# A two-layer transformer kernel: third normalisation, denominators and values reordered by halves on ScalarE and TensorE

## The chip, the cores and the metric

The kernel runs on one core of one Trainium2 chip. Time is device microseconds (us) of one launch; the time before is the median of three runs. A core has TensorE (PE, matrix products and transposes; PEld are its weight loads), VectorE (DVE), ScalarE (ACT), GpSimd (POOL) and SyncE (SP, which only issues DMAs here). The engines run their own instruction queues in order and wait for each other on semaphores.

## The reference, cut to what matters

32 independent items x[b] of 128 x 1024 pass through four residual stages, each behind a layer norm:

```python
x = x + _L0_xattn_ref(_layernorm(x), ctx_4096, ...)  # attention over 1024 positions
x = x + _L0_ffn_ref(_layernorm(x), ...)              # routed feed-forward, sign weights
x = x + _L1_xattn_ref(_layernorm(x), ctx_4096, ...)  # attention, 128 keys
x = x + _L1_ffn_ref(_layernorm(x), ...)              # routed low-rank feed-forward

# L0_xattn: q, k of 64 rows from ctx; attention = softmax(q k) over 1024 x 1024
v = jnp.einsum('oc,bct->bto', Wv, x) + bv
out = jnp.einsum('bts,bsc->bct', attention, v)
# L1_ffn
router_logits = jnp.einsum('bsd,hd->bsh', x, Wr) + br
scores = H * jax.nn.softmax(router_logits, axis=-1)
low = jnp.einsum('bsd,hrd->bshr', x, A)
out = SCALING * jnp.einsum('bshr,hor,bsh->bso', low, B, scores)
```

All is computed in float32, or in pairs of float32r parts (hi and lo) that together carry it.

## The kernel before, in words

After a setup of constants (transposed, split and multiplied weights) the kernel works on three items at a time, in a software pipeline. The body of iteration k does three kinds of work: **prepare** item b = k (load it, transpose its context, queries and keys, values), **attend** to item a = k-1 (the 1024 x 1024 attention of the first stage, in eight steps s), and **chain** for item c = k-2 (the second to fourth stages). `iterations` runs k = 0, 1, 2 written out, k = 3 to 31 in a loop, and k = 32 (attend and chain) and k = 33 (chain alone) written out. So thirty bodies, k = 2 to 31, hold all three kinds.

The order on each engine is the order in which its `body` is written; there is no scheduler. PSUM is full: `scores[0]`, `scores[1]`, `acc` (two banks each) and `shared[0]`, `shared[1]` (one bank each) pass from one use to the next, and the semaphores guard these passes.

The stretch that matters is the end of a body, after the last of the eight attention steps (line numbers are those of the kernel before):

- TensorE: transposes of `den_inv`, the reciprocal denominators, into `scores[1]` (L1192); transposes of the context `c_in` into `shared` (L1004), four per half; transposes of `xn_3`, the input of the fourth stage, into `shared` (L1004 again; `xn_3` is the buffer `p_sum`); `values(0)` and `values(1)` (L1010), eight small products of `xn` and `wvT` into `scores[1]`, four per half; the low-rank product with the router (L1213, `low_done`); first products of the next item's `kw` (L1037 to L1039); the transpose of `low` (L1219); the output products (L1224 to L1230). In this list a float32 matmul shows as two instructions.
- ScalarE: `den_rows` (the buffer `prob[0]`) from `scores[1]`, both halves (L729); `cT_hi` (L733); the third normalisation into `xn_3`, 1024 wide (`normalize(3, ...)`, L643); `cT_whole` (L740); the first half of `xnT` (L649); `v_hi` by halves (L748, L750); the router's exponential (L753).
- VectorE: statistics for the third normalisation (L774 to L779); `den_inv` (L935); `cT_lo` (L944); `x1_half(a, 0)` (L801, L802); the second half of `xnT` (L790); `x1_half(a, 1)`; statistics for the first normalisation of the attended item (L774 on); the router's softmax (L962 to L966) and `low` (L968).
- GpSimd turns the statistics into `rstd` and `shift` (`norm_scale`, L617, L618).

`half(h)` is the h-th 512 columns. `nth(per, b, n)` is the semaphore value after n of item b's `per` increments.

Of the kernel before, what the change touches and what calls it, by code (L numbers as in the profile page):

```python
# [21 lines left out]
ACT = mybir.ActivationFunctionType  # L22
# [26 lines left out]
def build(nc, x, ctx_, wq0, bq0, wk0, bk0, wv0, bv0, w_ffn, b_ffn, gate, ics, ocs,  # L49
# [13 lines left out]
    with top:  # L63
        def sb(name, shape, dt=F32, stack=top):
            return stack.enter_context(nc.sbuf_tensor(name, shape, dt))

        def sem(name, stack=top):
            return stack.enter_context(nc.semaphore(name))
# [36 lines left out]
        with ExitStack() as tmp:  # L105
# [62 lines left out]
            with nc.Block() as block:  # L168
                @block.sync
                def _(sp):  # L170
                    for i in range(4):
                        sp.dma_start(wq_nat[:, 2 * i:2 * i + 2, :],
                                     wq1[2 * i * P:(2 * i + 2) * P, :].rearrange("(t p) x -> p t x", p=P)).then_inc(wq_in[i], 16)
                    for i in range(2):
                        sp.dma_start((wf_first, wf_last)[i][:, :, :],
                                     w_ffn[4 * i * P:(4 * i + 4) * P, :].rearrange("(t p) h -> p t h", p=P)).then_inc(wf_in[i], 16)
                    for n, ft in enumerate(f_order):
                        sp.dma_start(of_tile(ft, wk_nat_split, wk_nat_whole),
                                     wk1[:, ft * P:(ft + 1) * P].rearrange("(t p) f -> p t f", p=P)).then_inc(wk_in[n], 16)
# [238 lines left out]
        den_rows = prob[0]  # L418
        unread = prob[1]

        res = sb("res", [P, D])
# [9 lines left out]
        rstd = [sb(f"rstd{i}", [P, 1]) for i in range(4)]  # L431
        shift = [sb(f"shift{i}", [P, 1]) for i in range(4)]
# [22 lines left out]
        def psum(name, shape):  # L455
            return top.enter_context(nc.psum_tensor(name, shape, F32))

        scores = [psum(f"scores{i}", [P, D]) for i in range(2)]
# [13 lines left out]
        shift_ready = [sem(f"shift_ready{i}") for i in range(4)]  # L472
        normed = [sem(f"normed{i}") for i in range(4)]
# [10 lines left out]
        den_done = sem("den_done")  # L484
        den_turned = sem("den_turned")
# [33 lines left out]
        den_rows_ready = sem("den_rows_ready")  # L519
        x1_ready = sem("x1_ready")  # L520
# [33 lines left out]
        def half(h):  # L554
            return slice(h * HALF, (h + 1) * HALF)
# [5 lines left out]
        def nth(per, b, n):  # L561

            if isinstance(b, int):
                return max(0, per * min(b, NB - 1) + n)
            return b * per + n


        def iterations(engine, body):  # L570
            for k in range(3):
                body(k, True, k >= 1, k >= 2)
            with engine.Fori(3, NB) as k:
                body(k, True, True, True)
            body(NB, False, True, True)
            body(NB + 1, False, False, True)

        with nc.Block() as block:
# [31 lines left out]
            @block.gpsimd  # L610
            def _(pool):
                def norm_scale(i, b):

                    pool.wait_ge(var_ready[i], nth(1, b, 1))
                    pool.wait_ge(normed[i], nth(1, b - 1, 1))
                    pool_norm[i].begin(b)
                    pool_norm[i].chain(pool, nc.gpsimd.tensor_tensor(rstd[i][:, :], var_eps[i][:, :], minus_half[:, :], ALU.pow))  # L617
                    nc.gpsimd.tensor_tensor(shift[i][:, :], neg_mean[i][:, :], rstd[i][:, :], ALU.mult).then_inc(shift_ready[i], 1)  # L618
                    pool_norm[i].end()

                def body(k, prepare, attend, chain):
                    b, a, c = k, k - 1, k - 2
                    if chain:
                        pool.wait_ge(x1_ready, nth(2, c, 2))
                        pool.wait_ge(out_ready, nth(2, c - 1, 2))
                        nc.gpsimd.tensor_tensor(res[:, :], x1[:, :], bias_rows[:, :], ALU.add).then_inc(biased, 1)
                    if chain:
                        norm_scale(2, c)
                    if prepare:
                        norm_scale(0, b)  # L630
                    if chain:
                        norm_scale(3, c)
                    if attend:
                        norm_scale(1, a)

                iterations(pool, body)
# [3 lines left out]
            def _(act):  # L640
                def normalize(i, b, to, src):
                    act.wait_ge(shift_ready[i], nth(1, b, 1))
                    nc.scalar.activation(to[:, :], src[:, :], ACT.Identity, bias=shift[i][:, :],  # L643
                                         scale=rstd[i][:, :]).then_inc(normed[i], 1)

                def transposed_half(i, c):

                    act.wait_ge(xnT_done[i], nth(2, c, 1))
                    nc.scalar.activation(tile4(xnT, 0), shared[0][:, :], ACT.Identity).then_inc(xnT_a_ready[i], 1)  # L649

                def body(k, prepare, attend, chain):
                    b, a, c = k, k - 1, k - 2
# [32 lines left out]
                    for s in range(T):  # L685
# [14 lines left out]
                        if chain and s == 3:  # L700
                            act.wait_ge(x2_ready, nth(2, c, 2))
                            normalize(2, c, xn_2, res)
# [15 lines left out]
                    if prepare:  # L718
                        for h in range(2):
                            act.wait_ge(qk_done, nth(2, b, h + 1))  # L720
                            nc.scalar.activation(q_hl[0:DQK, half(h)], scores[0][0:DQK, half(h)], ACT.Identity,
                                                 bias=bqk_col[0:DQK, :]).then_inc(q_hi_ready, 1)
                            nc.scalar.activation(k_hh[DQK:P, half(h)], scores[0][DQK:P, half(h)], ACT.Identity,
                                                 bias=bqk_col[DQK:P, :]).then_inc(k_hi_ready, 1)
                    if attend:
                        for h in range(2):
                            act.wait_ge(den_turned, nth(2, a, h + 1))
                            act.wait_ge(x1_ready, nth(2, a - 1, 2))
                            nc.scalar.activation(den_rows[:, half(h)], scores[1][:, half(h)], ACT.Identity).then_inc(den_rows_ready, 1)  # L729
                    if prepare:  # L730
                        act.wait_ge(cT_done, nth(2, b, 1))
                        act.wait_ge(kw_done, nth(2, b - 1, 2))
                        nc.scalar.activation(cT_hi[:, :, :].rearrange("p t c -> p (t c)"), shared[0][:, :],  # L733
                                             ACT.Identity).then_inc(cT_hi_ready, 1)
                    if chain:
                        act.wait_ge(den_done, nth(1, a, 1))
                        normalize(3, c, xn_3, res)
                    if prepare:
                        act.wait_ge(cT_done, nth(2, b, 2))
                        nc.scalar.activation(cT_whole[:, :, :].rearrange("p t c -> p (t c)"), shared[1][:, :],  # L740
                                             ACT.Identity).then_inc(cT_whole_ready, 1)
                    if chain:
                        act.wait_ge(sc1_done, nth(1, c, 1))
                        transposed_half(3, c)
# [251 lines left out]
            def _(pe):  # L996
# [3 lines left out]
                def transposes(h, src, semaphore):  # L1000

                    for j in range(4):
                        t = 4 * h + j
                        last = nc.tensor.transpose(shared[h][:, j * P:(j + 1) * P], src[:, t * P:(t + 1) * P], ident[:, :])  # L1004
                    last.then_inc(semaphore, 1)

                def values(h):

                    for t in range(4 * h, 4 * h + 4):
                        last = mm(scores[1][:, t * P:(t + 1) * P], xn[:, t * P:(t + 1) * P], wvT[:, :], start=True, stop=True)  # L1010
                    last.then_inc(v_done, 1)
# [71 lines left out]
                def body(k, prepare, attend, chain):  # L1083
                    b, a, c = k, k - 1, k - 2
# [110 lines left out]
                    if prepare:  # L1195
                        for h in range(2):
                            pe.wait_ge(x3_ready, nth(2, c, h + 1))
                            transposes(h, c_in, cT_done)
                    if chain:
                        pe.wait_ge(normed[3], nth(1, c, 1))  # L1200
                        for h in range(2):
                            pe.wait_ge((cT_lo_ready, cT_whole_ready)[h], nth(1, b, 1))
                            transposes(h, xn_3, xnT_done[3])
                    if prepare:
                        pe.wait_ge(normed[0], nth(1, b, 1))
                        pe.wait_ge(den_rows_ready, nth(2, a, 2))
                        values(0)
                        values(1)
                    if chain:
                        pe.wait_ge(xnT_a_ready[3], nth(1, c, 1))  # L1210
                        pe.wait_ge(xnT_b_ready[3], nth(1, c, 1))
# [44 lines left out]
```

## Time and profile before

| | us |
|---|---|
| median of three runs | 2334.17 (2333.06 to 2336.49) |
| profiled execution | 2332.57 |
| its span | 2330.8 |
| PE busy | 2175.6 (93%) |
| DVE busy | 1874.4 (80%) |
| ACT busy | 1113.5 (48%) |
| POOL busy | 260.2 (11%) |

The mean granted clock of TensorE over the span was 0.979 of full speed. Busy shares are means over the span. A wait shows in the trace as idle time ahead of an instruction, in square brackets with the instruction that released it. TensorE's matmuls are pipelined: the next one's start lies before the last one's end. The chain of waits is the sequence of work, one piece released by the other, that leads to the last instruction.

### The profile page before, as it was taken

The numbers are of one execution on the slowest core, as the hardware profiler recorded it, in microseconds if no ns is written. First come the engines' busy times: TensorE is split into PE (matmuls) and PEld (weight loads), VectorE is DVE, ScalarE is ACT, GpSimd is POOL, SyncE is SP. The second block draws the span as 40 slices with busy tenths as digits, with TensorE's granted clock in tenths as the row PEclk, the third lists the DMA queues.
The fourth block names the chain that finished last, engine by engine and source line by source line (L and its number), as shares of the span: only waits on it lengthen the run. The fifth ranks groups of instructions, "written<-read, shape, count | busy, mean of one in ns | idle before, by whom it ended". The sixth has DMA issues, their size and how long they took to land.

```text
span 2330.8 us, 34027 instructions
## 1 busy us (share of the span) xinstructions
PE 2175.6 (93%) x11166; PEld 1668.0 (72%) x11166; DVE 1874.4 (80%) x3130; ACT 1113.5 (48%) x1625; POOL 260.2 (11%) x302
## 2 busy tenths in 40 slices
PE   1997999999999999999999999999999999999996
PEld 0784777777777777777777777777777777777774
DVE  1436888988888888898888888898888888888873
ACT  1103545555555554555555544555555555455541
POOL 0000111111011111111011111111101111111100
PEclk7999999999999999999999999999999999999996
DMA  8001111111111111111111111111111111111100
GB/s 241 10 1 45 46 55 37 54 54 49 41 54 45 45 54 46 44 54 54 36 54 49 46 50 54 36 54 54 48 42 54 45 45 54 41 49 54 54 10 27
DMA packets 50217, 115.58 MB, mean 50 GB/s; under 512 B 14800, under 2 KB 23248, under 8 KB 50192
## 3 DMA queue, kind: packets, MB, share of 16 engines
q1 hardware_dynamic: 38624, 113.26, 14.8%
q10 hardware_dynamic: 11568, 1.98, 0.6%
q8 instruction: 16, 0.26, 0.0%
q14 instruction: 9, 0.07, 0.0%
HBM read 81.67 MB, written 16.78 MB: 42 GB/s over the span
## 4 chain that ended last, share of the span: by engine, by line
PE 85%; ACT 4%; issue 2%; DVE 2%; DMA 0%; POOL 0%; ACTq 0%; SPq 0%; POOLq 0%; DVEq 0%
PE acc L1080 15%; PE acc L1041 10%; PE scores L1024 5%; PE shared L1004 5%; PE shared L1054 5%; PE shared L1055 5%; PE scores L1069 5%; PE scores L1068 5%; PE shared L1213 3%; PE shared L1171 3%; PE acc L1037 3%; PE acc L1039 3%; PE acc L1038 3%; PE shared L1155 3%; PE scores L1182 2%; PE scores L1010 2%
## 5 line engine op out<-in xcount | busy, mean ns | idle before, releaser
L892 DVE TENSOR_TENSOR p_lo<-prob,p_hi 128x1024 fp32r<-128x1024 f32 x256 | 312.1, 1219 | 106.5 <-ACT p_hi L699 88.5
L692 ACT ACTIVATE prob<-scores 128x1024 f32<-128x1024 f32 x256 | 260.7, 1018 | 228.8 <-PE scores L1069 177.7
L785 DVE TENSOR_REDUCE neg_max<-scores 128x1 f32<-128x1024 f32 x256 | 312.0, 1219 | 38.1 <-PE scores L1024 32.7
L617 POOL TENSOR_TENSOR rstd<-var_eps,minus_half 128x1 f32<-128x1 f32 x128 | 127.0, 992 | 1883.7 <-DVE var_eps L779 1883.7
L699 ACT ACTIVATE p_hi<-prob 128x1024 fp32r<-128x1024 f32 x256 | 271.4, 1060 | 42.8 <-PE acc L1080 38.6
L1041 PE MATMUL acc<-m_whole,cT_whole 128*128 128x512 f32 x512 | 255.8, 601 | 0.0
L900 DVE TENSOR_TENSOR p_sum<-p_sum,prob 128x1024 f32<-128x1024 f32 x192 | 233.7, 1217 | 0.0
L1054 PE MATMUL shared<-signT,y_hi 128*128 128x512 f32 x512 | 206.6, 404 | 0.4 <-ACT oscale L681 0.4
L1068 PE MATMUL scores<-q_hl,k_hh 128*128 128x512 f32 x512 | 201.6, 394 | 1.8 <-DVE q_m L874 1.4
L1055 PE MATMUL shared<-signT,y_lo 128*128 128x512 f32 x512 | 202.5, 396 | 0.0
L1024 PE MATMUL scores<-k_hh,q_hl 128*128 128x512 f32 x512 | 202.3, 476 | 0.3 <-issue 0.3
L1069 PE MATMUL scores<-q_m,k_l 128*128 128x512 f32 x512 | 201.8, 394 | 0.0
L1080 PE MATMUL acc<-p_hi,v_hi 128*128 128x512 f32 x512 | 170.8, 415 | 4.1 <-DVE p_lo L892 3.9
L1080 PE MATMUL acc<-p_lo,v_hi 128*128 128x512 f32 x512 | 161.1, 395 | 0.0
L1080 PE MATMUL acc<-p_hi,v_lo 128*128 128x512 f32 x512 | 161.0, 395 | 0.0
L1024 PEld LDWEIGHTS scores<-k_hh,q_hl 128*128 128x128 f32 x512 | 94.2, 189 | 65.0 <-issue 46.6
L1004 PE MATMUL shared<-ident,p_sum 128*128 128x128 f32 x512 | 70.9, 283 | 57.5 <-ACT p_sum L643 57.5
L1041 PEld LDWEIGHTS acc<-m_whole,cT_whole 128*128 128x128 f32 x512 | 89.6, 189 | 44.3 <-issue 36.8
L1054 PEld LDWEIGHTS shared<-signT,y_hi 128*128 128x128 f32 x512 | 97.2, 190 | 26.8 <-DVE y_lo L808 0.9
L1068 PEld LDWEIGHTS scores<-q_hl,k_hh 128*128 128x128 f32 x512 | 96.1, 188 | 25.8 <-DVE q_m L874 1.8
L1037 PE MATMUL acc<-m_hi,cT_hi 128*128 128x512 f32 x256 | 109.5, 428 | 4.1 <-DVE cT_lo L944 2.2
L1080 PEld LDWEIGHTS acc<-p_lo,v_hi 128*128 128x128 f32 x512 | 96.0, 188 | 23.5
(221 smaller groups left out, 4301.4 us busy)
## 6 DMA issues: line engine op xcount, KB each, us to landing
c_in<-in_ctx SPq DMA_DIRECT2D x32, 512.0 KB, 3.3
xn<-in_x SPq DMA_DIRECT2D x32, 512.0 KB, 4.1
x<-in_x SPq DMA_DIRECT2D x32, 512.0 KB, 3.3
c_val<-in_ctx SPq DMA_DIRECT2D x32, 512.0 KB, 3.5
out_x<-oscale SPq DMA_DIRECT2D x32, 512.0 KB, 2.9
q_m<-q_hl SPq DMA_DIRECT2D x32, 256.0 KB, 3.1
k_hh<-k_hh SPq DMA_DIRECT2D x32, 256.0 KB, 3.4
wq_nat<-in_L_xattn_Wq SPq DMA_DIRECT2D x4, 1024.0 KB, 10.0
```

The source lines that it names most:

```text
L692: nc.scalar.activation(prob[s % 2][:, :], scores[s % 2][:, :], ACT.Exp).then_inc(exp_ready, 1)
L699: nc.scalar.activation(p_hi[s % 2][:, :], prob[s % 2][:, :], ACT.Identity).then_inc(p_hi_ready, 1)
L785: nc.vector.tensor_reduce(neg_max[:, t:t + 1], scores[t % 2][:, :], AX_X, ALU.max, negate=True).then_inc(row_max, 1)
L892: nc.vector.tensor_tensor(p_lo[s % 2][:, :], prob[s % 2][:, :], p_hi[s % 2][:, :].bitcast(F32), ALU.subtract).then_inc(p_lo_ready, 1)
L900: nc.vector.tensor_tensor(p_sum[:, :], p_sum[:, :], prob[s % 2][:, :], ALU.add).then_inc(p_summed, 1)
L1024: last = mm(scores[t % 2][:, half(h)], q_hl[:, t * P:(t + 1) * P], k_hh[:, half(h)], start=True, stop=True)
L1041: last = mm(acc[:, half(h)], cT_whole[:, f - TS, :], m_whole[:, f - TS, half(h)], start=f == 0, stop=f == T - 1)
L1054: mm(shared[h][:, :], y_hi[:, f, :], signT[:, f, half(h)], start=f == 0, stop=False)
L1055: last = mm(shared[h][:, :], y_lo[:, f, :], signT[:, f, half(h)], start=False, stop=f == T - 1)
L1068: mm(scores[s % 2][:, half(h)], k_hh[:, s * P:(s + 1) * P], q_hl[:, half(h)], start=True, stop=False)
L1069: last = mm(scores[s % 2][:, half(h)], k_l1[:, s * P:(s + 1) * P], q_m[:, half(h)], start=False, stop=True)
L1080: last = mm(acc[:, half(h)], v[:, s, :], p[s % 2][:, half(h)], start=first, stop=end)
```

## The change

ScalarE normalises `xn_3` in two halves of 512 columns. The first half comes ahead of the first half of the denominators' eviction, the second between `cT_hi` and `cT_whole`; the second half of the denominators comes behind `cT_whole`. TensorE computes `values(0)` ahead of the transposes of `xn_3` and `values(1)` behind them, each waiting for its own half of `den_rows`, and each half of the transposes waits for its own half of `xn_3`. The semaphore `normed[3]` now counts two per item, and GpSimd's wait on it follows.

```diff
@@ norm_scale, GpSimd
-                    pool.wait_ge(normed[i], nth(1, b - 1, 1))
+                    pool.wait_ge(normed[i], nth(2, b - 1, 2) if i == 3 else nth(1, b - 1, 1))
@@ helpers, ScalarE
+                def normalize_half(i, b, h, to, src):
+                    act.wait_ge(shift_ready[i], nth(1, b, 1))
+                    nc.scalar.activation(to[:, half(h)], src[:, half(h)], ACT.Identity, bias=shift[i][:, :],
+                                         scale=rstd[i][:, :]).then_inc(normed[i], 1)
+
+                def evict_den(a, h):
+                    act.wait_ge(den_turned, nth(2, a, h + 1))
+                    act.wait_ge(x1_ready, nth(2, a - 1, 2))
+                    nc.scalar.activation(den_rows[:, half(h)], scores[1][:, half(h)], ACT.Identity).then_inc(den_rows_ready, 1)
@@ body, ScalarE
-                    if attend:
-                        for h in range(2):
-                            act.wait_ge(den_turned, nth(2, a, h + 1))
-                            act.wait_ge(x1_ready, nth(2, a - 1, 2))
-                            nc.scalar.activation(den_rows[:, half(h)], scores[1][:, half(h)], ACT.Identity).then_inc(den_rows_ready, 1)
+                    if chain:
+                        act.wait_ge(den_done, nth(1, a, 1))
+                        normalize_half(3, c, 0, xn_3, res)
+                    if attend:
+                        evict_den(a, 0)
                     if prepare:
                         ...
                     if chain:
-                        act.wait_ge(den_done, nth(1, a, 1))
-                        normalize(3, c, xn_3, res)
+                        normalize_half(3, c, 1, xn_3, res)
                     if prepare:
                         ...
+                    if attend:
+                        evict_den(a, 1)
@@ values, TensorE
-                def values(h):
-
+                def values(h, a):
+                    pe.wait_ge(den_rows_ready, nth(2, a, h + 1))
@@ body, TensorE
-                    if chain:
-                        pe.wait_ge(normed[3], nth(1, c, 1))
+                    if prepare:
+                        pe.wait_ge(normed[0], nth(1, b, 1))
+                        values(0, a)
+                    if chain:
                         for h in range(2):
+                            pe.wait_ge(normed[3], nth(2, c, h + 1))
                             pe.wait_ge((cT_lo_ready, cT_whole_ready)[h], nth(1, b, 1))
                             transposes(h, xn_3, xnT_done[3])
                     if prepare:
-                        pe.wait_ge(normed[0], nth(1, b, 1))
-                        pe.wait_ge(den_rows_ready, nth(2, a, 2))
-                        values(0)
-                        values(1)
+                        values(1, a)
```

ScalarE's order in the loop's body before, from the last eviction of the keys on (`prob` is `den_rows`, `p_sum` is `xn_3`):

```order
L723 ACTIVATE k_hh<-scores,bqk_col 64x512
L729 ACTIVATE prob<-scores 128x512 [waits x1_ready,den_turned] x2
L733 ACTIVATE cT_hi<-shared 128x512 [waits kw_done,cT_done]
L643 ACTIVATE p_sum<-res,shift,rstd 128x1024 [waits shift_ready3,den_done]
L740 ACTIVATE cT_whole<-shared 128x512 [waits cT_done]
L649 ACTIVATE xnT<-shared 128x512 [waits xnT_done3,sc1_done]
```

And after the change:

```order
L733 ACTIVATE k_hh<-scores,bqk_col 64x512
L648 ACTIVATE p_sum<-res,shift,rstd 128x512 [waits shift_ready3,den_done]
L654 ACTIVATE prob<-scores 128x512 [waits x1_ready,den_turned]
L743 ACTIVATE cT_hi<-shared 128x512 [waits kw_done,cT_done]
L648 ACTIVATE p_sum<-res,shift,rstd 128x512 [waits shift_ready3]
L749 ACTIVATE cT_whole<-shared 128x512 [waits cT_done]
L654 ACTIVATE prob<-scores 128x512 [waits x1_ready,den_turned]
L659 ACTIVATE xnT<-shared 128x512 [waits xnT_done3,sc1_done]
```

One instruction of 1024 columns became two of 512, and the two denominators' evictions moved apart.

TensorE's order at the same place before, from the transposes of the context to the low-rank product:

```order
L1004 MATMUL shared<-ident,c_in 128x128 [waits x3_ready]
L1004 MATMUL shared<-ident,c_in 128x128 x3
L1004 MATMUL shared<-ident,p_sum 128x128 [waits cT_lo_ready,normed3]
L1004 MATMUL shared<-ident,p_sum 128x128 x3
L1004 MATMUL shared<-ident,p_sum 128x128 [waits cT_whole_ready]
L1004 MATMUL shared<-ident,p_sum 128x128 x3
L1010 MATMUL scores<-wvT,xn 128x128 [waits den_rows_ready,normed0]
L1010 MATMUL scores<-wvT,xn 128x128 x7
L1213 MATMUL shared<-lowT,xnT 128x136 [waits xnT_b_ready3,xnT_a_ready3]
```

And after:

```order
L1015 MATMUL shared<-ident,c_in 128x128 [waits x3_ready]
L1015 MATMUL shared<-ident,c_in 128x128 x3
L1021 MATMUL scores<-wvT,xn 128x128 [waits den_rows_ready,normed0]
L1021 MATMUL scores<-wvT,xn 128x128 x3
L1015 MATMUL shared<-ident,p_sum 128x128 [waits cT_lo_ready,normed3]
L1015 MATMUL shared<-ident,p_sum 128x128 x3
L1015 MATMUL shared<-ident,p_sum 128x128 [waits cT_whole_ready,normed3]
L1015 MATMUL shared<-ident,p_sum 128x128 x3
L1021 MATMUL scores<-wvT,xn 128x128 [waits den_rows_ready]
L1021 MATMUL scores<-wvT,xn 128x128 x3
L1224 MATMUL shared<-lowT,xnT 128x136 [waits xnT_b_ready3,xnT_a_ready3]
```

Half of the values moved ahead of the eight transposes, and one more wait stands in the row. VectorE's and SyncE's orders are as before.

## Rows read from the trace of the kernel before

**Rows 1.** The page, busy us, share of the span and instructions of each engine
```profile
PE 2175.6 (93%) x11166; PEld 1668.0 (72%) x11166; DVE 1874.4 (80%) x3130; ACT 1113.5 (48%) x1625; POOL 260.2 (11%) x302
```

**Rows 2.** The chain of waits, 1017 to 1036 us: start, us, what
```profile
1025.61 1.79 PE scores L1010 x16
1027.40 1.86 PE shared L1213 x16
1029.25 0.23 PE acc L1037
...
1031.35 0.11 PE shared L1219
```

**Rows 3.** Waits of the whole run: total us, times, longest
```profile
PE shared L1004 <- ACT p_sum L643: 57.5, 32, 4.9
```

**Rows 4.** Instructions in order of time, TensorE, 1009 to 1035 us
```profile
1021.79 1.04 PE L1004 MATMUL shared<-ident,c_in 128*128 128x128 f32 x8
1024.52 1.09 PE L1004 MATMUL shared<-ident,p_sum 128*128 128x128 f32 x8 [1.70 <-ACT p_sum L643]
```

**Rows 5.** The same, ScalarE
```profile
1021.55 1.09 ACT L729 ACTIVATE prob<-scores 128x512 f32<-128x512 f32 x2 [1.67 <-PE scores L1192]
1022.52 0.60 ACT L733 ACTIVATE cT_hi<-shared 128x512 fp32r<-128x512 f32 x1
1023.15 1.24 ACT L643 ACTIVATE p_sum<-res,shift,rstd 128x1024 f32<-128x1024 f32 x1
1024.30 0.58 ACT L740 ACTIVATE cT_whole<-shared 128x512 f32<-128x512 f32 x1
1025.27 0.60 ACT L649 ACTIVATE xnT<-shared 128x512 f32<-128x512 f32 x1 [0.40 <-PE shared L1004]
```

**Rows 6.** The same, VectorE
```profile
1023.16 0.69 DVE L944 TENSOR_TENSOR cT_lo<-shared,cT_hi 128x512 fp32r<-128x512 f32 x1 [1.48 <-ACT cT_hi L733]
...
1024.48 0.75 DVE L802 SCALAR_TENSOR_TENSOR x<-prob,bv_col,x 128x512 f32<-128x512 f32 x1
1025.65 0.69 DVE L790 COPY xnT<-shared 128x512 f32<-128x512 f32 x1 [0.42 <-PE shared L1004]
...
1029.47 0.16 DVE L962 TENSOR_TENSOR logit<-shared,br_rows 128x8 f32<-128x8 f32 x1
...
1030.76 0.29 DVE L968 TENSOR_TENSOR low<-shared,route 128x128 f32<-128x128 f32 x1
```

**Rows 7.** The same, GpSimd
```profile
1020.84 0.19 POOL L618 TENSOR_TENSOR shift<-neg_mean,rstd 128x1 f32<-128x1 f32 x1
```

**Rows 8.** Groups by line and shape, ScalarE: busy us, mean ns, idle before
```profile
L699 ACT ACTIVATE p_hi<-prob 128x1024 fp32r<-128x1024 f32 x256 | 271.4, 1060 | 42.8 <-PE acc L1080 38.6
...
L643 ACT ACTIVATE p_sum<-res,shift,rstd 128x1024 f32<-128x1024 f32 x32 | 39.7, 1240 | 6.4 <-POOL shift L618 5.6
...
L676 ACT ACTIVATE y_hi<-xnT 128x512 fp32r<-128x512 f32 x64 | 39.3, 631 | 72.2 <-DVE xnT L861 72.2
```

**Rows 9.** Instructions in order of time, last body (k = 33), GpSimd and ScalarE
```profile
2313.16 0.19 POOL L618 TENSOR_TENSOR shift<-neg_mean,rstd 128x1 f32<-128x1 f32 x1
2313.44 1.24 ACT L643 ACTIVATE p_sum<-res,shift,rstd 128x1024 f32<-128x1024 f32 x1 [5.63 <-POOL shift L618]
```

**Rows 10.** The same, body k = 32, TensorE
```profile
2258.05 1.91 PE L1192 MATMUL scores<-ident,den_inv 128*128 128x128 f32 x8
2261.77 1.97 PE L1004 MATMUL shared<-ident,p_sum 128*128 128x128 f32 x8 [1.81 <-ACT p_sum L643]
2264.61 3.83 PE L1213 MATMUL shared<-lowT,xnT 128*128 128x136 f32 x16 [0.87 <-DVE xnT L790]
```

**Rows 11.** The same, VectorE
```profile
2263.78 0.69 DVE L790 COPY xnT<-shared 128x512 f32<-128x512 f32 x1 [2.43 <-PE shared L1004]
```

**Rows 12.** Stretches: us, busy (instructions) of PE, PEld, DVE, ACT, POOL, PEclk, DMA
```profile
1021.00:1025.00 4.00, 2.30 (x21) 2.07 (x20) 2.49 (x5) 3.30 (x5) 0.02 (x1) 1.00 0.31 87
2260.00:2265.00 5.00, 2.35 (x10) 1.99 (x11) 2.53 (x4) 2.32 (x3) 0.00 (x0) 0.50 0.00 0
```

## The prediction

> **What bounds the kernel now.** I read the page first. TensorE is busy for 93% of the span and VectorE for 80% [rows 1]. A change that takes no work away can gain only where TensorE stands idle, or where VectorE hands it something late. The waits of the whole run say where: the transposes of `xn_3` wait for ScalarE's normalisation in all 32 bodies, 57.5 us together [rows 3]. In a body of the loop that is one gap of 1.70 us, from the end of the context's transposes at 1022.83 to 1024.52 [rows 4]. It is the only long gap of a body, and the change is aimed at it. Thirty bodies (k = 2 to 31) have all three kinds of work and show this stretch alike; the two after them differ and are priced apart.
>
> Then the order of time on each engine, to see who is late. ScalarE evicts the denominators from 1021.55 (it had idled 1.67 us), `cT_hi` from 1022.52, normalises from 1023.15 to 1024.39, and `cT_whole` follows at 1024.30 [rows 5]. TensorE starts 0.13 us after the normalisation's end; that is the hand-over I use. The shift that the normalisation needs was ready at 1021.03 [rows 7], two microseconds earlier: it waits only for its turn on ScalarE.
>
> The chain of waits then stays on TensorE: transposes, values (1.79 us), low-rank product (1.86), first products for the next item from 1029.25, the transpose of `low` from 1031.35 [rows 2]. But VectorE is close beside it. From `cT_lo` on, its only idle time up to the router is 0.42 us ahead of its copy of the second half of `xnT` at 1025.65 [rows 6]. After that come `x1_half`, the statistics and the router without a gap until `logit` at 1029.47, and `low` ends at 31.05 (1030.76 + 0.29), just 0.3 us before its transpose [rows 2, 6]. So whatever TensorE wins in front of `low`, it loses again waiting for `low`, unless VectorE becomes earlier too. That decides the size of the gain.
>
> **The change part by part**, at the body around 1023; all times from here are us behind 1000.
>
> *First half on ScalarE.* In the last body the shift ends at 2313.35 and the normalisation starts at 2313.44 [rows 9], so the first half starts at 21.03 + 0.09 = 21.12. The trace has no normalisation of 512 columns. A plain copy from SBUF takes 1060 ns for 1024 columns and 631 for 512; the normalisation takes 1240 for 1024, 180 more than the plain copy [rows 8]. I take 631 + 180 = 0.81 us. Bounds: 0.62 (half of 1.24, no fixed part) and 1.24 (no gain from the halving). Neighbours on ScalarE overlap by 0.09 (24.30 against 24.39) [rows 5]. So the denominators' first half starts at 21.12 + 0.81 - 0.09 = 21.84 instead of 21.55; two of them started 0.97 apart from `cT_hi` [rows 5], so one takes 0.49, and `cT_hi` could start at 22.33. It needs the first four transposes of `c_in`, which start at 21.79 [rows 4]; four transposes reach ScalarE after 0.75 us (24.52 to 25.27) [rows 4, 5], that is at 22.54. So `cT_hi` keeps its start, 22.52, with 0.2 us of cover, and costs nothing. Without that cover (a half over 1.0 us) everything behind moves by the excess.
>
> *VectorE ahead of the transposes.* `cT_lo` waits for `cT_hi` and stays at 23.16. `x1_half(a, 0)` follows it and ends at 25.23 as before [rows 6]; its half of the denominators is ready at about 22.4, its cover is `cT_lo`.
>
> *`values(0)` on TensorE.* Half of 1.79, 0.90 us, starts at once at 22.83 (denominators' half 0 evicted by then) and ends at 23.73. The transposes' first half waits for `cT_lo` as before, 23.85 + 0.13 = 23.98. So `values(0)` lies wholly in the old gap and delays nothing.
>
> *Second half on ScalarE and second transposes.* The normalisation's second half starts at 23.15 and ends at 23.96, `cT_whole` runs from 23.87 to 24.45, and the second transposes, which wait for it, start at 24.58, against about 25.15 before. If they start on an idle engine, VectorE sees them 0.75 later, at 25.33; if they follow the first four without a break (these end at about 24.60), VectorE sees them 1.13 after 23.98, as before (24.52 to 25.65), at 25.11 [rows 4, 6]. VectorE is free at 25.23. So its copy starts at 25.23 to 25.33 instead of 25.65: 0.32 to 0.42 earlier, and I take 0.37.
>
> The Trainium skill speaks against halving: "Advanced Engine Details and Errata", section "The Read-Write Bubble", says that on ScalarE and VectorE the memory latency is exposed between instructions, so that large tiles are cheaper. The two plain copies agree: 2 x 631 - 1060 = 202 ns are paid per instruction [rows 8]. With that fixed part the half is 0.81 and the end is 25.33; without it the half is 0.62 and VectorE's own 25.23 binds. It costs at most 0.1 us a body, since only one half lies on the path.
>
> *Behind the transposes.* The denominators' second half runs on ScalarE from 24.36 to 24.96, `values(1)` from about 25.09 to 26.0, and `xnT` is whole on VectorE at 25.28 + 0.69 = 25.97. The low-rank product starts at about 26.1 and not 27.40: TensorE is here 1.3 us early. `x1_half(a, 1)` needs the denominators' second half at 25.9, which is covered. TensorE's first products (2.1 us, 29.25 to 31.35) then end at 26.1 + 1.86 + 2.1 = 30.06. But VectorE's row is only 0.37 earlier: `low` ends at 30.68, its transpose starts at about 30.8. TensorE idles some 0.7 us there. So of 1.3 us it keeps about 0.4: the gap of 1.70 is split, not filled, and what is late next is `low`. After that both engines run as before, 0.37 earlier, into the next body, where every wait is for TensorE or VectorE themselves. The semaphore's new count on GpSimd is met long before it is asked for.
>
> *Body k = 32.* There is no `cT_hi` or `values`. The transposes started at 2261.77 behind ScalarE's row; the denominators' transposes ended at 2259.96. The first half of the normalisation is done by then, the second by about 2260.5. TensorE can go on at about 2260.0, and the copy of `xnT` that started at 2263.78 comes at about 2262.1: 1.7 us [rows 10, 11]. Bounds: 0 and 1.81, the gap. *Body k = 33:* the transposes start after 0.81 instead of 1.24 [rows 8, 9]: 0.4 us.
>
> *Sum.* 30 x 0.37 + 1.7 + 0.4 = 13.2 us. The profiled execution took 2332.57, so it would take 2319.4. The median of the runs shown is 1.6 above it, 2334.17, so I predict 2321.0. The two ends of the forecast's own term are 0.25 (a hand-over or a restart of TensorE more than counted) and 0.50 (VectorE's 0.42, and the transpose of `low` no longer queued behind a matmul): 9.6 and 17.1 us, so 2325 and 2317.
>
> **The rivals.**
>
> *The second transposes are not earlier (no change).* They wait for `cT_whole`, which still stands behind a normalisation half. For 0.32 us of gain the half must take 0.81; at 1.0 us VectorE is at 25.52 and the gain is 0.13 a body, 30 x 0.13 + 1.5 = 5 us: 2329. For it speaks that the half was never measured; against it, 631 ns for the plain copy. 2329 to 2334.
>
> *TensorE keeps all of its lead.* If `low` didn't bind, a body would gain 1.3 us: 30 x 1.3 + 2 = 41, 2293. Against it stands VectorE's gapless row from 25.65 to `logit` [rows 6].
>
> *Slower: halves that cost as much as the whole.* At 1.24 us each, the denominators start at 22.27, `cT_hi` at 22.76 (0.24 late), `cT_lo` follows, the second half of the normalisation runs 23.39 to 24.63, `cT_whole` to 25.12, the second transposes start at 25.25, and VectorE copies at 26.00 instead of 25.65. That is 30 x 0.35 = 10.5 us, less about 1 in the last bodies: 2344. It turns into a loss from a half of about 1.07 us on. Only the 1024-wide row supports it; the 631 ns speak against it [rows 8].
>
> *Slower: TensorE's clock.* The gap becomes several short ones. In the present body the clock stays at 1.00 (2.4 GHz) through a gap of 1.70 us [rows 12]. In k = 32 it is 0.50 (1.2 GHz) [rows 12], and it had fallen before that body's gap of 1.81: the eight transposes ahead of it took 1.91 us, eight of the same shape in the loop 1.04 [rows 4, 10]. At the lower level transposes take 1.97 against 1.09 and the low-rank product 3.83 against 1.86 [rows 2, 4, 10]; with values at twice 1.79 that is 9.4 us from 22.83, 32.2 instead of 29.25, 3.0 us a body: 2334 + 89 = 2423. Idle time in the stretch gets less, not more, so I give it little. The Trainium skill has such a case in "TensorE: Matmul & The Clock Gate", section "A second HAM failure mode: psum-queue depth-cycling": short idles between groups of matmuls made the clock go up and down.
>
> **How the numbers follow.** Forecast 75%, the second transposes not earlier 13%, TensorE keeps all 3%, costly halves 5%, clock 4%. The 0.2% that a measurement of this kernel can tell from no change is 4.7 us. Of the 13% about 6 still gain more than that. So faster is 75 + 3 + 6 = 84%, within 0.2% 8%, slower 8% (the last two rivals, less a mild form of either). Range: the forecast's own 2317 to 2325, widened below to 2314 for a stretch that gains 0.6 a body, above to 2329 for a half of 1.0 us.
>
> **What would show it.** In the profile after: the normalisation in halves of about 810 ns; `cT_hi` and `cT_lo` at the same distance as now; the idle time ahead of VectorE's copy of `xnT` down from 0.42 to about 0.1; the low-rank product about 1.3 us earlier against `cT_hi`, the transpose of `low` only about 0.4; a new wait of TensorE for `low`, 0.6 to 0.7 us in thirty bodies, some 20 us in all; and TensorE's wait for `xn_3` near nothing in the loop. I am wrong in size if `logit` no longer follows the statistics without a gap, or if the second transposes come later than 25.2; wrong in sign if a half takes over 1.07 us or the clock in the loop falls below 1.00.

## The result and the profile after

The changed kernel takes 2312.55 us (median of four runs, 2311.51 to 2312.75) against 2335.16 us for the kernel before in the same session (2333.06 to 2336.49). The ratio is 0.9907, 95% interval 0.9894 to 0.9919: 21.7 us less, where 13.2 were forecast. The sign was right; the time lies 1.5 us below the range.

The profiled execution has a span of 2310.7 us, 20.1 less than before. Here is where they are, taken at the start of `cT_hi` on ScalarE, which every body with prepare has once:

| us | before | after |
|---|---|---|
| start to `cT_hi` of k = 2 | 305.98 | 309.54 |
| from there to k = 31 (29 bodies) | 1889.36 | 1871.62 |
| one of these bodies | 65.15 | 64.54 |
| from there to the end | 135.43 | 129.54 |

The bodies with all three kinds of work are 0.61 us shorter each, not 0.37; in either kernel the 29 intervals lie within 0.1 us of each other. The first and last bodies move by several us in opposite directions; more on them below.

TensorE in the body around 1020, in order of time (start us, us, engine, line, operation, shapes, count, idle before and its releaser); it answers to [rows 4] and [rows 2]:

```profile
1017.91 1.04 PE L1203 MATMUL scores<-ident,den_inv 128*128 128x128 f32 x8
1018.78 1.04 PE L1015 MATMUL shared<-ident,c_in 128*128 128x128 f32 x8
1019.70 1.13 PE L1021 MATMUL scores<-wvT,xn 128*128 128x128 f32 x8
1020.91 1.09 PE L1015 MATMUL shared<-ident,p_sum 128*128 128x128 f32 x8
1021.84 1.09 PE L1021 MATMUL scores<-wvT,xn 128*128 128x128 f32 x8
1022.90 2.09 PE L1224 MATMUL shared<-lowT,xnT 128*128 128x136 f32 x16
...
1027.50 0.33 PE L1230 MATMUL shared<-ident,low 128*128 128x128 f32 x1 [0.41 <-DVE low L979]
```

The low-rank product and `low`'s transpose in the kernel before, whose denominators' transposes start at 1020.92:

```profile
1027.23 2.02 PE L1213 MATMUL shared<-lowT,xnT 128*128 128x136 f32 x16
...
1031.19 0.27 PE L1219 MATMUL shared<-ident,low 128*128 128x128 f32 x1
```

The gap of 1.70 us is gone. From the start of the denominators' transposes to that of the low-rank product it is now 4.99 us and was 6.31, but a new wait of 0.41 us stands ahead of `low`'s transpose. ([rows 2], and with them the prediction, have 1027.40 and 1031.35. Those are starts of pieces of the chain, which begin where the matmul ahead ends; the instructions themselves start 0.17 and 0.16 earlier.) The transposes of `xn_3` run as one group of eight: the second four did not start anew.

ScalarE, for [rows 5]:

```profile
1018.12 0.81 ACT L648 ACTIVATE p_sum<-res,shift,rstd 128x512 f32<-128x512 f32 x1 [1.24 <-POOL shift L618]
1018.96 0.60 ACT L654 ACTIVATE prob<-scores 128x512 f32<-128x512 f32 x1
1019.45 0.59 ACT L743 ACTIVATE cT_hi<-shared 128x512 fp32r<-128x512 f32 x1
1019.93 0.81 ACT L648 ACTIVATE p_sum<-res,shift,rstd 128x512 f32<-128x512 f32 x1
1020.63 0.60 ACT L749 ACTIVATE cT_whole<-shared 128x512 f32<-128x512 f32 x1
1021.11 0.61 ACT L654 ACTIVATE prob<-scores 128x512 f32<-128x512 f32 x1
```

A half takes 0.81 us, as worked out. But `cT_hi` comes 1.54 us behind the denominators' transposes and not 1.60, and the second half overlaps `cT_hi`'s end by 0.11, where the whole normalisation had started 0.03 behind it [rows 5].

VectorE, for [rows 6]:

```profile
1020.07 0.69 DVE L955 TENSOR_TENSOR cT_lo<-shared,cT_hi 128x512 fp32r<-128x512 f32 x1 [1.39 <-ACT cT_hi L743]
...
1021.40 0.75 DVE L813 SCALAR_TENSOR_TENSOR x<-prob,bv_col,x 128x512 f32<-128x512 f32 x1
1022.07 0.68 DVE L801 COPY xnT<-shared 128x512 f32<-128x512 f32 x1
...
1025.87 0.16 DVE L973 TENSOR_TENSOR logit<-shared,br_rows 128x8 f32<-128x8 f32 x1
...
1026.69 0.16 DVE L976 RECIPROCAL r_inv<-r_sum 128x1 f32<-128x1 f32 x1 [0.46 <-ACT r_exp L764]
...
1027.15 0.29 DVE L979 TENSOR_TENSOR low<-shared,route 128x128 f32<-128x128 f32 x1
```

There is no bracket left ahead of the copy of `xnT`: VectorE's row is without a gap from `cT_lo` to `logit`. The copy starts 0.08 before its neighbour ends (1022.15). In the chain of waits of this stretch (start us, us, what), TensorE has handed over to VectorE:

```profile
1019.55 0.50 ACT cT_hi L743
...
1020.68 0.69 DVE prob L812
...
1021.40 0.69 DVE x L813
1022.09 0.66 DVE xnT L801
...
1027.15 0.30 DVE low L979
...
1027.50 0.33 PE shared L1230
```

Before, ScalarE's normalisation and then TensorE alone stood there, up to `low`'s transpose:

```profile
1023.15 1.25 ACT p_sum L643
...
1024.52 1.09 PE shared L1004 x8
```

In the whole run VectorE has 9% of the chain now and had 2%.

How VectorE's row reaches the next body is seen at its end. The values' remainders (`v_lo`) are read out of `scores[1]`, and TensorE's next product into `scores[1]`, which belongs to the next body, waits for them. VectorE, TensorE's weight load, and that wait in the whole run:

```profile
1029.37 1.29 DVE L994 TENSOR_TENSOR v_lo<-scores,v_hi 128x512 fp32r<-128x512 f32 x2
1030.72 0.19 PEld L1035 LDWEIGHTS scores<-k_hh,q_hl 128*128 128x128 f32 x1 [0.30 <-DVE v_lo L994]
PEld scores L1035 <- DVE v_lo L994: 9.3, 31, 0.5
```

### The profile page after: what moved, and what is told of

It is laid out like the page before. It is cut to its first block, busy times and chain, and to the rows that moved or that the text cites. A ratio compares the mean times of both kernels' runs of the same rounds, so it can differ in the third digit from the quotient of the medians.

```text
span 2310.7 us, 34120 instructions
## 1 busy us (share of the span) xinstructions
PE 2193.5 (95%) x11166; PEld 1672.1 (72%) x11166; DVE 1872.3 (81%) x3130; ACT 1116.4 (48%) x1657; POOL 259.9 (11%) x302
## 4 chain that ended last, share of the span: by engine, by line
PE 77%; DVE 9%; issue 3%; ACT 2%; POOL 0%; DMA 0%; DVEq 0%; SPq 0%; POOLq 0%; ACTq 0%
PE acc L1091 15%; PE acc L1052 10%; PE scores L1035 5%; PE shared L1065 5%; PE shared L1066 5%; PE scores L1080 5%; PE scores L1079 5%; PE shared L1015 4%; PE shared L1182 3%; PE shared L1166 3%; PE scores L1193 2%; PE scores L1187 2%; DVE x L813 2%; DVE prob L812 2%; PE acc L1048 2%
## 5 line engine op out<-in xcount | busy, mean ns | idle before, releaser
L1080 PEld LDWEIGHTS scores<-q_m,k_l 128*128 128x128 f32 x512 | 96.1, 188 | 23.0
```

Source lines behind the costliest of these rows:

```text
L1080: last = mm(scores[s % 2][:, half(h)], k_l1[:, s * P:(s + 1) * P], q_m[:, half(h)], start=False, stop=True)
```

## The experiments

All are compared with the kernel before, run beside them: it took 2333.20 us beside e1 to e4, 2334.07 beside e5 to e8, and 2334.84 beside e9 and e10. "A body" is the mean over the 29 intervals from k = 2 to 31 in the profile. The last two columns are distances from the start of the denominators' transposes in the body around 1020.

| | median us | ratio (95%) | a body | copy of `xnT` | `low` |
|---|---|---|---|---|---|
| before | 2335.16 | | 65.15 | 4.73 | 9.84 |
| after | 2312.55 | 0.9907 (0.9894 to 0.9919) | 64.54 | 4.16 | 9.24 |
| e1_act_only | 2313.43 | 0.9918 (0.9905 to 0.9932) | 64.54 | 4.15 | 9.24 |
| e2_pe_only | 2332.43 | 0.9997 (0.9988 to 1.0006) | 65.10 | 4.71 | 9.80 |
| e3_pad_after | 2323.59 | 0.9958 (0.9944 to 0.9971) | 64.86 | 4.48 | 9.57 |
| e4_pad_before | 2333.81 | 1.0004 (0.9995 to 1.0013) | 65.14 | 4.74 | 9.83 |
| e7_whole_ahead | 2327.03 | 0.9972 (0.9961 to 0.9983) | 64.97 | 4.58 | 9.67 |
| e8_halves_behind | 2336.97 | 1.0014 (1.0005 to 1.0023) | 65.34 | 4.95 | 10.05 |
| e5_router | 2301.67 | 0.9859 (0.9843 to 0.9875) | 64.23 | 4.14 | 8.56 |
| e6_router_before | 2345.36 | 1.0052 (1.0038 to 1.0065) | 65.50 | 4.74 | 9.84 |
| e9_router_values_late | 2323.29 | 0.9955 (0.9941 to 0.9968) | 64.90 | 4.15 | 9.23 |
| e10_stats_later | 2303.86 | 0.9867 (0.9852 to 0.9883) | 64.25 | 4.15 | 8.58 |

**Which part does it: e1_act_only and e2_pe_only.** Each half of the change alone.

```diff
@@ e1, from after, TensorE: values back behind the transposes
-                        values(0, a)
                     if chain: ... transposes(h, xn_3, xnT_done[3])
                     if prepare:
+                        values(0, a)
                         values(1, a)
@@ e2, from before, TensorE: values(0, a) ahead, values(1, a) behind, ScalarE untouched
```

> The kernel after, but with both halves of the values behind the transposes of xn_3 on TensorE, as before the change; ScalarE's new order and its halves stay. Theory: VectorE's gapless row sets the gain as long as TensorE stays in front of it. TensorE's part is then 0.90 us later at the low-rank product: in the profile after it would end its first products at 1027.75 instead of waiting until 1027.50 for low, so 0.25 to 0.35 us a body are lost: 2312.5 + 9 = 2321 (2318 to 2324). Rival 1, only ScalarE's order counts: 2312 to 2314. Rival 2, the gain is the TensorE work that was put into the gap (0.9 us a body): the gain is gone, 2334 to 2339.

> The kernel before, with TensorE's part of the change alone: the first half of the values ahead of the transposes of xn_3, each half waiting for its own half of the denominators. ScalarE as before. Theory: VectorE's copy of xnT still waits for the whole normalisation, low is as late as before, so at most 0.1 us a body: 2332 to 2336. Rival 1 (only ScalarE's order counts): the same, 2335. Rival 2, the filled gap is the gain: 0.9 us x 30 = 27 less, 2308.

The first expectation missed (2318 to 2324 us, measured 2313.43). The low-rank product is 0.72 us later than in the kernel after, as it had to be, and the body is the same to 0.01 us. Its profile, TensorE in order of time:

```profile
1017.00 1.03 PE L1203 MATMUL scores<-ident,den_inv 128*128 128x128 f32 x8
...
1022.71 2.02 PE L1223 MATMUL shared<-lowT,xnT 128*128 128x136 f32 x16
...
1026.66 0.28 PE L1229 MATMUL shared<-ident,low 128*128 128x128 f32 x1
```

`low`'s transpose comes 9.66 behind the start against 9.59: TensorE just arrives when `low` does. So TensorE's half of the change, which fills the gap one sees, is worth nothing by itself: in the loop 0.003 us a body on top of ScalarE's half, and 0.05 alone, which the timed runs cannot tell from nothing (0.9988 to 1.0006). In e2 the low-rank product is 0.77 us earlier than in the kernel before (5.54 against 6.31), and TensorE loses it in a wait for `low`:

```profile
1032.73 0.33 PE L1219 MATMUL shared<-ident,low 128*128 128x128 f32 x1 [0.41 <-DVE low L968]
```

Rival 2, that the work put into the gap is the gain, is refuted in both directions. Rival 1, that only ScalarE's order counts, holds in both kernels.

**Is VectorE's row the bound: e3_pad_after and e4_pad_before.** The same addition in both kernels, ahead of the copy of `xnT`:

```diff
+                    if prepare and chain:
+                        nc.vector.tensor_tensor(pad[:, :], bias_rows[:, 0:256], bias_rows[:, 0:256], ALU.add)
                     if chain:
                         transposed_half(3, c)
```

> The kernel after, with one more addition of 256 columns on VectorE (about 0.35 us) ahead of the copy of the second half of xnT, in the thirty bodies of all three kinds. Theory: VectorE's row is the bound, so it costs its whole length, 30 x 0.3 to 0.4 = 9 to 12 us: 2322 to 2325. Rival, TensorE or ScalarE is the bound in this stretch: 0 to 2 us, 2312 to 2315.

> The kernel before, with the same added addition of 256 columns on VectorE. Theory: VectorE waits 0.42 us there for TensorE's transposes, and a released instruction misses another 0.08 of overlap with its neighbour, so an addition of 0.35 us is hidden: 0 to 2 us, 2335 to 2337. Rival, VectorE was the bound already before the change: 9 to 12 us, 2344 to 2347.

In the profile of e3 the addition, in order of time on VectorE, takes its slot:

```profile
1024.10 0.75 DVE L814 SCALAR_TENSOR_TENSOR x<-prob,bv_col,x 128x512 f32<-128x512 f32 x1
1024.77 0.42 DVE L964 TENSOR_TENSOR pad<-bias_rows 128x256 f32<-128x256 f32 x1
1025.10 0.68 DVE L802 COPY xnT<-shared 128x512 f32<-128x512 f32 x1
```

It moves the copy by 0.33 us and the body by 0.32 (64.54 to 64.86). Before the change it costs nothing measurable (65.15 to 65.14). Both costs are as expected; e4's time lies 1.2 us under the range given for it because the kernel before, beside it, took 2333.20 and not 2335; the difference is 0.6. The change put the part of VectorE's row ahead of the copy on the path, and the slack that it used up was at least 0.33 us.

**Which of ScalarE's moves: e7_whole_ahead and e8_halves_behind.** Early but whole; halved but not early.

```diff
@@ e7, from after, ScalarE (and the counts of normed[3] back to one)
-                        normalize_half(3, c, 0, xn_3, res)
+                        normalize(3, c, xn_3, res)
...
-                        normalize_half(3, c, 1, xn_3, res)
@@ e8, from after, ScalarE
-                        normalize_half(3, c, 0, xn_3, res)
                         evict_den(a, 0)
                         ... cT_hi ...
+                        normalize_half(3, c, 0, xn_3, res)
                         normalize_half(3, c, 1, xn_3, res)
```

> The kernel after, but the third normalisation is one instruction of 1024 columns again, where its first half stood (ahead of the denominators' first half); all the rest as after. Theory (what counts is when VectorE's row starts, by cT_hi, and that the second transposes are ready when it is free): the normalisation holds ScalarE from 18.12 to 19.36 in the profile after, cT_hi comes at about 19.88 instead of 19.45, so VectorE's row is 0.4 us later; a body takes 64.9 to 65.0 us instead of 64.54, the kernel 2322 to 2327. Rival, only the early start of the normalisation counts: 2312 to 2315.

> The kernel after, but both halves of the normalisation stand behind cT_hi and ahead of cT_whole; the denominators' first half is ahead of cT_hi again, their second half last. Theory: cT_hi is as early as after, but cT_whole and with it the second transposes wait for two halves, about 1.4 us behind cT_hi's end, and VectorE copies xnT at about the distance of before: a body of 65.0 to 65.2 us, 2330 to 2336. Rival, the halving itself or the late second half of the denominators is the gain: 2312 to 2320.

e7, ScalarE in order of time:

```profile
1019.92 1.24 ACT L643 ACTIVATE p_sum<-res,shift,rstd 128x1024 f32<-128x1024 f32 x1 [1.24 <-POOL shift L618]
1021.19 0.60 ACT L654 ACTIVATE prob<-scores 128x512 f32<-128x512 f32 x1
1021.68 0.59 ACT L743 ACTIVATE cT_hi<-shared 128x512 fp32r<-128x512 f32 x1
```

`cT_hi` starts 1.76 us behind the normalisation's start instead of 1.33: 0.43 later, and the body is 0.43 longer than after. It keeps 0.18 of the 0.61 us, as its expectation said (64.9 to 65.0 us a body). e8 has `cT_hi` early, but the copy of `xnT` waits again, on VectorE:

```profile
1026.61 0.69 DVE L800 COPY xnT<-shared 128x512 f32<-128x512 f32 x1 [0.73 <-PE shared L1014]
```

Its body is 0.19 longer than before. Body and time had been expected at 65.0 to 65.2 and 2330 to 2336 us, and lie 0.14 and 1 us above the upper ends. So neither an early normalisation nor a halved one is the gain by itself: the halves pay because one of them fits into ScalarE's idle time ahead of the denominators without delaying `cT_hi`.

In the eight kernels in which VectorE's row behind the copy is the same (before, after, e1 to e4, e7, e8), the body is the copy's distance plus 60.38 to 60.42 us. In all twelve it is the distance from the denominators' transposes to the end of the values' remainders (a mean over the bodies) plus 51.77 to 51.81 us, although that distance goes from 12.46 (e5) to 13.73 (e6), and TensorE's product into `scores[1]` starts 0.05 to 0.06 us behind that end. So the end of VectorE's row sets the body, before the change and after it.

**What binds behind the copy: e5_router and e6_router_before.** VectorE's order, from after and from before; nothing is left out:

```diff
                         dve.wait_ge(x1_ready, nth(2, a, 2))
-                        statistics(dve_attend, 1, a, x1)
+                        first half of bn_stats
                         logit, its maximum
+                        second half of bn_stats   (while ScalarE does the exponential)
                         reciprocal, route1, low
+                        bn_aggr, neg_mean, var_eps
```

> The kernel after, with VectorE's row behind x1_half(a, 1) reordered and nothing left out: first half of the statistics, then logit and its maximum, then the second half of the statistics while ScalarE does the exponential, then the rest of the router with low, then the end of the statistics. Theory: low, not TensorE, is what is late, so low is about 0.6 us earlier (27.15 to 26.5 in the profile after), and 0.46 us of VectorE's waiting for the exponential are filled: TensorE keeps 0.3 to 0.45 us a body, 2299 to 2304. Rival, the end of VectorE's row (the values' remainders) or TensorE is the bound and low was not: 2310 to 2314.

> The kernel before, with the same reordering of VectorE's row. Theory: before the change the low-rank product ends at 1029.25, later than logit would now be asked for (about 1028.5), so VectorE waits and low comes at most 0.1 us earlier; TensorE was no later than low there: at most 0.15 us a body, 2329 to 2334. Rival, VectorE's row is the bound with or without the change: 0.3 to 0.45 us a body, 2320 to 2325.

e5 is the fastest kernel of the study, 2301.67 us, some 11 us below the kernel after. On VectorE the wait for the exponential is filled and `logit` waits 0.16 for the low-rank product:

```profile
1022.35 0.69 DVE L795 BATCH_NORM_STATS2 stat<-x 128x6 f32<-128x512 f32 x1
1023.21 0.17 DVE L985 TENSOR_TENSOR logit<-shared,br_rows 128x8 f32<-128x8 f32 x1 [0.16 <-PE shared L1242]
1023.41 0.16 DVE L986 TENSOR_REDUCE r_max<-logit 128x1 f32<-128x8 f32 x1
1023.49 0.68 DVE L797 BATCH_NORM_STATS2 stat<-x 128x6 f32<-128x512 f32 x1
1024.21 0.16 DVE L991 RECIPROCAL r_inv<-r_sum 128x1 f32<-128x1 f32 x1
```

`low` is 0.68 us earlier, its transpose 0.59 (9.00 against 9.59), but the body only 0.31: the values' remainders at the end of VectorE's row, which TensorE waits for in the next body, start 0.30 earlier (11.16 against 11.46). So the end of the row counts and not `low`. The expectation met the time (2299 to 2304) and the 0.3 us a body, but not for the reason it gave, that `low` is what is late: the body follows the row's end. e6 shows it from the other side, and its expectation missed in sign. `logit` finds the low-rank product not done:

```profile
1036.40 0.17 DVE L974 TENSOR_TENSOR logit<-shared,br_rows 128x8 f32<-128x8 f32 x1 [0.84 <-PE shared L1231]
```

`low` is where it was (9.84), and yet the body is 0.35 longer: the waiting time in the row, 0.84 us, outweighs what is filled (0.46), and the start of the row's last two operations is 0.37 late (12.43 against 12.06). The kernel is 11 us slower than before, where up to 5 us less had been expected.

**When does the order of the values pay: e9_router_values_late; and the rest of the row: e10_stats_later.** e9 is e5 with both halves of the values behind the transposes (TensorE's part of the diff of e1). e10 is e5 with `bn_aggr, neg_mean, var_eps` behind the remainder of `lowT`.

> The kernel after with VectorE's reordered row (router between the halves of the statistics), and both halves of the values behind the transposes on TensorE, as before the change. Theory: in this row logit is asked for about 0.7 us earlier, so the 0.7 us by which the order of the values moves the low-rank product is no longer hidden: logit waits for it, VectorE's row and a body are 0.4 to 0.7 us longer than with the values split (64.23), 64.6 to 64.9, the kernel 2313 to 2322. Rival, the order of the values never matters (it moved the body by 0.003 us under the old row): 2300 to 2304.

> The kernel after with VectorE's reordered row, and the last three small operations of the statistics moved behind the remainder of lowT. Theory: VectorE's row has the same length, so its end (the values' remainders) stays and with it the body, 64.2; only TensorE's wait of about 0.12 us for lowT's remainder goes: 0 to 0.1 us a body, 2298 to 2303. Rival, low's transpose and the output products are the bound and not the row's end: 0.12 to 0.4 us a body, 2290 to 2298.

e9's body is 0.67 us longer than e5's (64.90 against 64.23), the upper end of the expectation, and its time, 2323.29 us, 1.3 us above it: `logit` waits again, on VectorE,

```profile
1028.88 0.17 DVE L985 TENSOR_TENSOR logit<-shared,br_rows 128x8 f32<-128x8 f32 x1 [0.81 <-PE shared L1241]
```

The same order of the values that was worth 0.003 us a body under the old row is worth 0.67 under the new one. e10 is no better than e5 (64.25 against 64.23 a body; its 2303.86 us are 0.9 above the range): TensorE's last short wait in front of the output products was not on the path.

## Why the prediction was right in sign and wrong in size

*The gap and what takes its place.* Right. The 1.70 us are gone, the low-rank product is early (4.99 against 6.31 us behind the denominators' transposes, 1.3 earlier, as forecast), and half of it is lost again: `low`'s transpose is only 0.69 earlier. The wait for `low` is 0.41 us in the trace's bracket, 0.6 to 0.7 forecast, since `low` itself came 0.60 earlier and not 0.37.

*The half of the normalisation.* Right: 0.81 us. `cT_hi` is not delayed; e7 shows the price of delaying it. Two halves hold ScalarE 0.38 us longer than one whole normalisation (2 x 0.81 against 1.24), and none of it lies on the path, where up to 0.1 us a body had been allowed for.

*The step that failed* is the copy of `xnT`: "0.32 to 0.42 earlier, and I take 0.37". It came 0.57 earlier against the denominators' transposes. Three small things were mis-sized. The lower end (0.32) rested on the second transposes starting anew; they ran on from the first, so the full 0.42 of idle time went, where the 0.37 is the middle of both cases. An instruction that is not held by a wait starts 0.08 before its neighbour ends, which the idle time in brackets does not contain (1022.07 against 1022.15). And `cT_hi` was not quite held by the context's transposes: with one eviction ahead of it and not two, VectorE's row began 0.08 earlier (2.16 against 2.24). In e8, where `cT_hi` does wait for those transposes, it starts 1.51 us behind the denominators', against 1.60 before and 1.54 after:

```profile
1023.17 0.60 ACT L740 ACTIVATE cT_hi<-shared 128x512 fp32r<-128x512 f32 x1 [0.28 <-PE shared L1014]
```

Together 0.58. The body then shortened by 0.61, since VectorE's row sets it; 30 x 0.24 = 7 of the 8.5 us of the miss are this term.

*The size of TensorE's part.* I let `values(0)` count as what fills the gap, and did not ask whether it mattered with VectorE's row as the bound. By e1 it does not: 9.66 against 9.59 for `low`'s transpose, and no difference behind. The argument from VectorE's row was the right one, and was not carried to its end.

*Body k = 32.* From `cT_hi` of k = 31 to `logit` of k = 32 it was 73.14 us and is 70.13: 3.0 less, of which 0.5 belong to the end of body 31. That is 2.5 against 1.7 forecast. The stretch from `logit` to `logit` takes 65.7 to 66.6 us in the four kernels with ScalarE's old order (before, e2, e4, e6) and 62.8 to 64.3 in the eight others, so the gain is real, and the means are 2.5 apart too; one pair of profiles gives it to about 1 us. ScalarE, in order of time:

```profile
2244.09 0.81 ACT L648 ACTIVATE p_sum<-res,shift,rstd 128x512 f32<-128x512 f32 x1 [6.58 <-POOL shift L618]
2244.81 0.58 ACT L654 ACTIVATE prob<-scores 128x512 f32<-128x512 f32 x1
2245.29 0.80 ACT L648 ACTIVATE p_sum<-res,shift,rstd 128x512 f32<-128x512 f32 x1
```

TensorE's clock differs in this body from what [rows 10] and [rows 12] have. The denominators' transposes, ahead of everything that the change moves in this body, take 1.06 us where [rows 10] have 1.91:

```profile
2243.30 1.06 PE L1203 MATMUL scores<-ident,den_inv 128*128 128x128 f32 x8
```

The granted clock in the stretch with most of the transposes of `xn_3` and the start of the low-rank product was 0.82, where [rows 12] have 0.50 (us, busy and count of PE, PEld, DVE, ACT, POOL, clock, DMA, GB/s):

```profile
2245.00:2250.00 5.00, 3.53 (x20) 3.08 (x21) 4.38 (x7) 2.06 (x4) 0.00 (x0) 0.82 0.00 0
```

How the 0.8 us above the forecast divide between the clock and the order was not tried.

*The last body and the first.* From `logit` to `logit` the last body took 53.10 us before and 50.21 after. But the same stretch takes 50.2 to 52.6 us in the seven kernels that normalise there in halves (after, e1, e3, e5, e8, e9, e10) and 52.3 to 53.1 in the five that don't, so the 0.4 us forecast for it can be neither confirmed nor refuted here. The first bodies took 3.6 us longer in the profile after, 2.9 of them between the first and the second `cT_hi`, where the code is unchanged. The granted clock differs there. The kernel before and after, from 195 to 200 us, the same columns:

```profile
195.00:200.00 5.00, 5.00 (x20) 3.55 (x20) 3.84 (x6) 0.24 (x1) 0.00 (x0) 1.00 0.82 261
```

```profile
195.00:200.00 5.00, 4.56 (x14) 3.58 (x15) 2.90 (x5) 0.93 (x2) 0.00 (x0) 0.68 0.88 279
```

*The rivals.* Costly halves: no, 0.81 us. Clock in the loop: no, its mean from 320 to 2150 us is 1.00 before and after. TensorE keeps all: no. Second transposes not earlier: no in the kernel after, but that is what e8 does.

*Sum.* 0.61 x 30 = 18.3 us, and with 2.5 for body k = 32 it is 20.8; measured 21.7 by the ratio. The 0.9 left over are less than what the first and last bodies differ by from one execution to the next, and no run divides them. The range was widened to 2314 for 0.6 us a body, so it all but held the loop's gain; body k = 32 and what is left over took the time past it.

## What to carry to other kernels

A gap on the busiest engine is worth only what the next late producer allows: before filling it, write down that producer's own row, and ask what starts it, what lengthens it, and who waits for its end. Here half of the edit filled the visible gap and was worth nothing as long as `logit` was asked for late in VectorE's row; once it was asked for earlier (e5), the same half was worth 0.67 us a body. Where an operation must go ahead of another on a queue, a half that fits into idle time can go there while a whole one delays what it passes.

## What the runs showed of the hardware that was not expected

A VectorE instruction that follows another without a wait mostly starts 0.06 to 0.09 us before the record of the first ends (`xnT` at 1022.07 against 1022.15), so a removed wait gives back that much more than its bracket. Where it reads what the one ahead wrote it mostly starts 0.03 to 0.04 behind the end instead (`x1_half`'s second operation at 1021.40 against 1021.36). On ScalarE `cT_whole` starts 0.11 before the end of the half ahead of it, while the denominators' first half starts 0.03 behind the end of its neighbour, which it does not read; why is not settled.

TensorE's granted clock in the unchanged first body was 1.00 in one execution and 0.68 in another. The start up to k = 2 took between 304.5 us (e8) and 311.2 (e5) over the twelve kernels profiled here, with mean clocks of 0.97 and 0.93 from 180 to 310 us, which is as much as thirty bodies gain from 0.2 us each. The period of equal bodies tells such kernels apart better than their spans do.
